# A graph network on one core: how four opening stages share their work among the engines

## The reference

```python
h = relu(layernorm(x))                                    # 625 x 512
# layer 0: mean of the neighbours, then one linear layer over [h, mean]
mean = segment_sum(h[src], dst, 625) / max(count, 1)
x = x + concat([h, mean]) @ W.T + b
# layer 1: two relational convolutions; layer 2: equivariant messages; layer 3: edge MLP with tail
# layer 1's weights of an edge: comp0[edge_type] * edge_weight and comp1[edge_type] * edge_weight
```

## Time and profile before

| | us |
|---|---|
| median of 3 runs | 2427.84 |
| lowest, highest | 2423.5, 2429.47 |
| the profiled execution | 2443.93 |
| its span in the trace | 2442.2 |
| PE busy / DVE / ACT / POOL | 2087.2 / 1827.6 / 1417.6 / 1259.0 |
| mean granted TensorE clock | 0.934 of 2.4 GHz |

### The profile page before, as it was taken

How to read it: one execution, slowest core, us unless ns; L and a number is a source line. 1 busy time by engine, 2 the same in 40 slices (tenths; PEclk the granted TensorE clock), 3 DMA queues, 4 the chain that set the end, 5 groups by cost and what they waited for, 6 DMA issues and landing times. The chain is left out here.

```text
span 2442.2 us, 38939 instructions
## 1 busy us (share of the span) xinstructions
PE 2087.2 (85%) x11291; PEld 1137.6 (47%) x11410; DVE 1827.6 (75%) x3717; ACT 1417.6 (58%) x2251; POOL 1259.0 (52%) x1060
## 2 busy tenths in 40 slices
PE   0567568888998886999999998799999999999965
PEld 0334257764665553444444445345555554555422
DVE  8658979965333344999999984699999999999723
ACT  2558667742112222444444442699999999999731
POOL 0572367741881004333333311588888888888530
PEclk9758889988999996999999999999999999999987
DMA  3310010010214324433333311332222222222000
GB/s 127 142 27 8 0 53 0 0 56 30 75 40 120 110 73 149 122 94 99 88 89 99 93 36 53 111 111 76 76 74 77 73 77 73 75 75 74 12 0 21
DMA packets 81554, 170.20 MB, mean 70 GB/s; under 512 B 17379, under 2 KB 43222, under 8 KB 80450
## 3 DMA queue, kind: packets, MB, share of 16 engines
q0 software_dynamic: 35840, 98.88, 14.9%
q1 hardware_dynamic: 45624, 70.25, 8.7%
HBM read 144.93 MB, written 23.98 MB: 69 GB/s over the span
## 5 line engine op out<-in xcount | busy, mean ns | idle before, releaser
L831 PE MATMUL e_two_ps<-w,e_first 128*128 128x512 bf16 x1342 | 407.8, 382 | 4.1 <-issue 0.2
L593 POOL DMA_INDIRECT sorted_records<-edge_record,slot_row x160 | 209.9, 1312 | 123.8 <-POOLq L731 60.2
L831 PE MATMUL e_two_ps<-w,e_first_low 128*128 128x512 bf16 x685 | 261.9, 382 | 0.6
L1678 POOL TENSOR_TENSOR e_first_low<-e_first 128x1024 bf16<-128x1024 f32 x88 | 250.3, 2844 | 21.8 <-DVE e_first L1869 21.8
L1683 POOL TENSOR_TENSOR e_msg_low<-e_act 128x1024 bf16<-128x1024 f32 x88 | 225.8, 2566 | 58.0 <-DVE e_act L1881 56.8
L1515 ACT ACTIVATE u_msg<-u_t,slot_record 128x128 f32<-128x128 f32 x528 | 172.9, 391 | 97.7 <-DVE u_t L1554 88.3
L2174 POOL DMA_INDIRECT e_got<-src_table,e_idx x176 | 186.7, 1061 | 70.4 <-POOL e_idx L2168 34.8
L1434 POOL DMA_INDIRECT u_got<-up_table,u_idx x176 | 168.9, 960 | 76.8 <-issue 42.9
L831 PEld LDWEIGHTS e_two_ps<-w,e_first 128*128 128x128 bf16 x1408 | 134.9, 98 | 150.2 <-issue 4.9
L1480 PE MATMUL u_sum_ps<-u_msg,u_hot 128*125 128x512 f32 x352 | 189.8, 621 | 15.4 <-DVE u_msg L1571 14.8
L635 PE MATMUL pairs_ps<-cell_high,src_hot 128*128 128x144 bf16 x1180 | 154.1, 228 | 43.7 <-POOL cell_rest L659 22.0
(11 more groups left out here) (349 smaller groups left out, 5275.3 us busy)
## 6 DMA issues: line engine op xcount, KB each, us to landing
conv_w<-in_L_gnn_basis_dram SPq DMA_DIRECT2D x8, 1024.0 KB
sorted_records<-pairs SPq DMA_DIRECT2D x5, 1408.0 KB, 10.9
edge_record<-in_edge_floats_dram SPq DMA_DIRECT2D x2, 3125.0 KB
later_w<-in_L_gnn_W_dram SPq DMA_DIRECT2D x6, 1024.0 KB
attr_parts<-h SPq DMA_DIRECT2D x22, 256.0 KB, 2.1
e_attrT<-attr_parts SPq DMA_DIRECT2D x44, 128.0 KB
e_dst_all<-dst_row SPq DMA_DIRECT2D x44, 125.0 KB
pairs<-in_edge_floats_dram SPq DMA_DIRECT2D x1, 3125.0 KB
```

The lines of the kernel that those rows point to most:

```text
L593: pg.nc.gpsimd.indirect_dma_start(out=pg.sorted, out_offset=bass.IndirectOffsetOnAxis(ap=pg.slot_row[:, j:j + 1], axis=0), in_=pg.edge_rec ...
L831: last = nc.tensor.matmul(out, lhsT, rhs, start=(n == 0), stop=(n == len(pairs) - 1))
L1678: nc.gpsimd.tensor_tensor(first_low[:, r % 2, 2 * u:2 * u + 2, :], full, upper(full), ALU.subtract).then_inc(low1, 1)
```

## The change

It has four parts. In place_edges the sum over buckets is done by 40 fused instructions and a tree of additions, two of its additions on POOL, ahead of POOL's work on the weights; the block tables move to POOL. In order_pairs the clearing of `pairs` is begun later and shared in other proportions, the coefficients' high parts are made on ACT, their rests on DVE, and the statistics of `x` are taken there. In build_pairs ACT makes `h`. In layer0 there is one block, and the counts, the means and the transposes of `h` work on bf16 halves.

```diff
@@ place_edges, POOL
+            pool.wait_ge(sem["group_compared"], 1)
+            nc.gpsimd.tensor_tensor(group_past[:, 0:2, :], group_past[:, 0:2, :], group_past[:, 2:4, :],
+                                    ALU.add).then_inc(sem["group_compared"], 1)
...
+            pool.wait_ge(sem["quarter_slots"], 2)
+            nc.gpsimd.tensor_tensor(pg.bucket_slot[:, 0:QUARTER, :], pg.bucket_slot[:, 0:QUARTER, :],
+                                    pg.bucket_slot[:, QUARTER:2 * QUARTER, :], ALU.add).then_inc(sem["slots_added"], 1)
+            pool.wait_ge(sem["slots_added"], 1)
+            pool.wait_ge(sem["quarter_slots"], 3)
+            nc.gpsimd.tensor_tensor(pg.bucket_slot[:, 0:QUARTER, :], pg.bucket_slot[:, 0:QUARTER, :],
+                                    pg.bucket_slot[:, 2 * QUARTER:3 * QUARTER, :], ALU.add)\
+                .then_inc(sem["slots_added"], 1)
@@ place_edges, ACT: the copies of the edge ends (late_ends) move behind the weights
@@ place_edges, DVE
-            link(nc.vector.tensor_tensor(rank[:, :, :], rank[:, :, :], over_j(shift[0:EP, :]), ALU.add))
-            link(nc.vector.tensor_tensor(pg.bucket_slot[:, :, :].rearrange("p j b -> p b j"), rank[:, :, :],
-                                         mine[:, :, :], ALU.mult))
-            link(nc.vector.tensor_reduce(slot[:, :], pg.bucket_slot[:, :, :], AX.X, ALU.add))
+            for b in range(BUCKETS):
+                last = nc.vector.scalar_tensor_tensor(out=pg.bucket_slot[:, b, :], in0=rank[:, b, :],
+                                                      scalar=shift[0:EP, b:b + 1], in1=mine[:, b, :],
+                                                      op0=ALU.add, op1=ALU.mult)
+                if b % QUARTER == QUARTER - 1:
+                    last.then_inc(sem["quarter_slots"], 1)
+            dve.wait_ge(sem["quarter_slots"], BUCKETS // QUARTER)
+            dve.wait_ge(sem["slots_added"], 2)
+            link(nc.vector.tensor_tensor(pg.bucket_slot[:, 0:QUARTER, :], pg.bucket_slot[:, 0:QUARTER, :],
+                                         pg.bucket_slot[:, 3 * QUARTER:4 * QUARTER, :], ALU.add))
+            left = QUARTER
+            while left > 2:
...
-            link(nc.vector.tensor_scalar(group_blk[:, :], group_no[:, :], last_group[:, 0:1], None, ALU.is_ge))
...
-            link(nc.vector.tensor_scalar(reached[:, :], item_last[:, :], pg.lane_no[:, 0:1], None, ALU.is_le))
-            nc.vector.tensor_reduce(bucket_of[:, :], reached[:, :], AX.X, ALU.add).then_inc(sem["tables_made"], 1)
@@ (these two now stand behind item_last, one compare for all blocks behind last_group)
@@ order_pairs, POOL
-            pool.wait_ge(placed, 1)
+            pool.wait_ge(decoded, 1)
...
-            for n in range(1, 4):
+            for n in range(1, 3):
                 nc.gpsimd.memset(pairs[:, n * size:(n + 1) * size], 0.0)
-            pool.wait_ge(high_early, 1)
-            nc.gpsimd.tensor_tensor(pg.pair_rest[:, :, 0:BASES].rearrange("p t n -> p n t"), coef[:, :, :],
-                                    pg.pair_high[:, :, 0:BASES].rearrange("p t n -> p n t"), ALU.subtract)
@@ order_pairs, ACT
+            act.wait_ge(x_var, 1)
+            nc.scalar.sqrt(x_sd[:, :], x_sd[:, :]).then_inc(x_root, 1)
             act.wait_ge(pg.emptied, 16 * 5)
...
+            nc.scalar.activation(pairs[:, 3 * size:], pg.ones[:, 0:1].broadcast_to([P, size]), ACT.Copy, scale=0.0)
             for m in range(2):
+                act.wait_ge(coefs_made, m + 1)
+                at = slice(2 * m, 2 * m + 2)
+                nc.scalar.copy(pg.pair_high[:, :, at].rearrange("p t n -> p n t"), coef[:, at, :]).then_inc(high_early, 1)
                 act.wait_ge(terms_read, 2 * (RELS - 1) + m + 1)
                 nc.scalar.copy(pg.pair_high[:, :, BASES + 2 * m:BASES + 2 * m + 2], later_coefs(m)).then_inc(high_late, 1)
@@ order_pairs, DVE
+            dve.wait_ge(pg.x_in, 16)
+            for b in range(NB):
+                last = nc.vector.bn_stats(out=pg.x_stats[:, b, :], in_=pg.x[:, b, :])
...
+            nc.vector.tensor_scalar(x_sd[:, :], x_mv[:, :, 1], EPS, None, ALU.add).then_inc(x_var, 1)
             dve.wait_ge(placed, 1)
...
+            for n in range(BASES):
+                last = nc.vector.tensor_scalar(coef[:, n, :], masks[:, first, :], ...)
+            link(last)
+            dve.sem_inc(decoded, 1)
             for r in RELS_IN_ORDER[2:]:
                 mask(r)
...
+            for m in range(2):
+                for k, r in enumerate(RELS_IN_ORDER[1:]):
+                    for n in range(2 * m, 2 * m + 2):
...                                         # scalar_tensor_tensor as before, linked after each pair
+            for m in range(2):
+                at = slice(2 * m, 2 * m + 2)
+                dve.wait_ge(high_early, m + 1)
+                nc.vector.tensor_tensor(pg.pair_rest[:, :, at].rearrange("p t n -> p n t"), coef[:, at, :],
+                                        pg.pair_high[:, :, at].rearrange("p t n -> p n t"), ALU.subtract)
@@ build_pairs, ACT, behind the last operand
+            for b in range(NB):
+                nc.scalar.activation(pg.h[:, b, :], pg.x[:, b, :], ACT.Relu, bias=pg.x_nmr[:, b:b + 1],
+                                     scale=pg.x_rs[:, b:b + 1])
@@ layer0
-        normalize(pg, "n0", sp_work=load, pe_work=counts, halves=True)
...
+                accumulate(nc, mean_ps[b % 2][:, :], [
+                    pair for sb in range(NB) for pair in three_products(
+                        linked_columns(0, sb, b), linked_columns(1, sb, b), h_parts[0][:, sb, :], h_parts[1][:, sb, :])])\
+                    .then_inc(made, 1)
+            def turn(b):
+                if b >= 2:
+                    pe.wait_ge(h_high, b - 1)
+                    pe.wait_ge(h_taken, b - 1)
+                for a in range(2):
+                    for f in range(4):
+                        last = nc.tensor.transpose(h_ps[b % 2][:, a, f, 0:BN], h_parts[a][:, b, f * P:(f + 1) * P],
+                                                   pg.ident16[0:BN, 0:BN])
+                last.then_inc(h_turned, 1)
...
+            pe.wait_ge(counts_early, 1)
+            pe.wait_ge(counts_late, 1)
+            for b in range(NB):
+                accumulate(nc, count_ps[:, b:b + 1], [(linked_columns(a, sb, b), pg.ones16[0:BN, :])
+                                                      for sb in range(NB) for a in range(2)]).then_inc(counted, 1)
+            pe.wait_ge(h_low, 1)
             mean(0)
+            for b in range(NB):
+                turn(b)
@@ layer0, ACT copies the high half of each turned block, DVE the low half (h_turned_low)
@@ layer0, POOL and DVE: the low half of the count matrix, 2 and 3 of its 5 sets; DVE: the low half of h
+            nc.gpsimd.tensor_tensor(linked[1][:, at, :], pg.pairs[0:BN, at, COEFS, :], linked[0][:, at, :],
+                                    ALU.subtract).then_inc(counts_late, 1)
...
+            nc.vector.tensor_tensor(linked[1][:, at, :], pg.pairs[0:BN, at, COEFS, :], linked[0][:, at, :],
+                                    ALU.subtract).then_inc(counts_early, 1)
+            nc.vector.tensor_tensor(h_parts[1][:, :, :], pg.h[:, :, :], h_parts[0][:, :, :], ALU.subtract).then_inc(h_low, 1)
```

More of the change, by code:

```diff
@@ L78, in constants @@
     pg.before = pg.sb("before", [P, P])
+    pg.ones16 = pg.sb("ones16", [P, 1], BF16)
     pg.ln2 = pg.sb("ln2", [P, 1])
@@ L251, in _ @@
                 nc.scalar.copy(pg.weight_part[:, n, :], weight_16[:, n, :]).then_inc(sem["weight_part"], 1)
+            for n, at in ((0, slice(0, EARLY)), (1, slice(EARLY, EC))):
+                ends = pg.late_ends if n else pg.edge_record[0:EP, 0:EARLY, SRC:SRC + 2]
+                nc.scalar.copy(ends[:, :, 0], ints[:, 0, at])
+                nc.scalar.activation(ends[:, :, 1], ints[:, 1, at], ACT.Identity, bias=pg.ones[0:EP, 0:1])
         @block.tensor
@@ L564, in _ @@
             link(nc.vector.tensor_copy(pg.pair_high[:, :, COEFS], filled[:, :]))
+            first = RELS_IN_ORDER[0]
+            dve.wait_ge(x_root, 1)
+            nc.vector.reciprocal(pg.x_rs[:, :], x_sd[:, :]).then_inc(x_chain, 1)
+            dve.wait_ge(x_chain, 3)
+            nc.vector.scalar_tensor_tensor(out=pg.x_nmr[:, :], in0=x_mv[:, :, 0], scalar=-1.0, in1=pg.x_rs[:, :],
+                                           op0=ALU.mult, op1=ALU.mult)
+            dve.wait_ge(comp_in, 32)
+            for n in range(BASES):
+                last = nc.vector.tensor_scalar(coef[:, n, :], masks[:, first, :],
+                                               comp[:, 0, first * BASES + n:first * BASES + n + 1], None, ALU.mult)
+            link(last)
+            dve.sem_inc(decoded, 1)
             for r in RELS_IN_ORDER[2:]:
@@ L993, in _ @@
             for b in range(NB):
+                act.wait_ge(h_turned, b + 1)
+                nc.scalar.copy(hT[:, 0, :, nodes_of(b)], h_ps[b % 2][:, 0, :, 0:BN]).then_inc(h_high, 1)
+            for b in range(NB):
```

(2 more changed lines are left out.)

124 lines of the change are left out of this document (76 added, 48 removed).

## The result

| | before | changed |
|---|---|---|
| median, us (4 runs each) | 2426.38 | 2406.47 |
| lowest, highest | 2423.5, 2429.47 | 2405.49, 2410.63 |
| ratio, with 95% interval | | 0.9921 [0.9903, 0.9939] |
| span of the profiled execution | 2442.2 | 2404.3 |
| mean granted clock in it | 0.934 | 0.947 |

A forecast was written before the change was run, and what follows sets the result against it. Each block was taken to cost what its last engine needs: DVE in place_edges, ACT behind the loop, PE in the first layer. 4.9 + 8.7 - 0.95 + 4.4 = 17.0 us off 2427.84 gave 2410.8, range 2400 to 2420.

The forecast's parts named there:

- place_edges: Sum over buckets: DVE stays the bound, POOL's additions add to its time, DVE ends at 65.05, 4.9 us saved.
- The carry through the loop: order_pairs' loop: begun earlier, it ends earlier by as much, so place_edges' 4.9 us carry through.
- Behind the loop: End of order_pairs: ACT is late, its second clearing on the path; block ends at 309.2, 8.7 us saved.
- build_pairs: ACT's five added relus end 0.95 us behind DVE; cost 0.95 us, 1.7 at most.
- layer0: First layer, timed from its start T: product(0) ends at T + 33.2, later means shorter; 4.4 us saved.
- The rule on transposes: First layer: transposes don't count as busy for the clock gate, so the clock falls and mean(1) costs 6.0 us.
- The first: Rival, first layer: clock stays up through counts, mean and transposes, saving 11.3 us; 2403.9 us, chance 0.15.
- The second: Rival, order_pairs: POOL's memsets hold back DVE's masks, pair_cell and coefficients; 2415.7 us, chance 0.16.
- The third: Rival, place_edges: POOL's additions cost L442's price, block ends 2.2 us later than before; 2417.9 us, chance 0.08.
- The fourth: Rival, first layer: the one block doesn't shorten it; 2415.2 us, chance 0.11.
- the slower one: Rival, first layer: PE stays at the low clock, 7.4 us more a block, 2452 us with all five; chance 0.03.
- my own mark: First layer: the prediction called itself wrong if product(0) ended before T + 30, T being the layer's start.

The follow-up runs named there:

- e5: The changed kernel with POOL's two additions of slots (1600 elements each) done by DVE instead; 2406.92 us, ratio to before 0.9926.
- e1: The kernel before, unchanged, profiled a second time, on another chip; 2382.67 us (1 run).
- e2: The kernel before with the changed place_edges alone; 2380.27 us, ratio to before 0.9996.
- e3: The changed kernel with the clearing of before: three memsets on POOL once the slots are placed, one clearing on ACT; 2365.18 us, ratio to before 0.9941.
- e4: The changed kernel with the old first layer and norm, without statistics of x in order_pairs or relu in build_pairs; 2366.37 us, ratio to before 0.9941.
- e0: The changed kernel again, no edit, on a later chip; 2407.26 us, ratio to before 0.9929.
- e8: The changed kernel with early high copies and rests of the coefficients walked in the outputs' memory order; 2403.04 us, ratio to before 0.9915.
- e11: The changed kernel with the first layer's 50 bf16 count products issued six times over; 2411.74 us (1 run).
- e7: The changed kernel with each block of h transposed three times over, 24 bf16 transposes instead of 8; 2407.20 us (1 run).
- e6: The changed kernel with the last quarter of the clearing moved from ACT to POOL, three memsets there; 2398.29 us, ratio to before 0.9891.

## Why the prediction was right, and where it wasn't

The time and its range held (2406.5 in 2400 to 2420, forecast 2410.8), and the direction. Step by step:

- **place_edges.** Right, to 0.45 us. The terms came out (12.0 and 11.92; two additions on POOL, 7.8 forecast, 3.4 and 3.56 once they ran; 65.05 and 65.48 at the end), because the two engines' times were added and not overlapped. e5 shows what that means: the shared work is worse than DVE alone, by 2.05 us.
- **The carry through the loop.** Against e1 the loop ends 4.7 us earlier in e2, 4.1 in e3 and 3.8 in e4, where it began 4.6, 4.35 and 4.3 earlier. On the other kind of chip the loop's length differs by 5 us from one execution of the changed kernel to the next, and only one profile of the kernel before is there; whether all 4.45 us arrive there is open. The stretches without the loop give 4.45 + 5.8 - 0.8 + 12.15 = 21.6 us; the medians 19.9 and 17.5 (e0). The 2 to 4 us between are unsettled.
- **Behind the loop.** The path was right (through ACT, second clearing on it, copies begin at 285.96, 32.5 us after the slots as forecast). The size of the term "four copies at 0.95 us, two rests at 0.86" was wrong: 6.06 us and, for the rests behind the last copy, 2.46 us. I had taken rows whose outputs I hadn't looked at for their order. In e8, with the outputs in the order of memory, the stretch is 4.1 us shorter. So 5.8 instead of 8.7 us.
- **build_pairs.** +0.8, forecast +0.95.
- **layer0.** The step that failed: 12.15 us instead of 4.4. Its terms: the counts (T + 11.0 forecast for their end, T + 6.0 found; they and DVE's halves together are 3.3 us, since the counts are hidden behind L1147 and cost 0.030 us each and not the 0.108 of an fp32 pass); mean(0) 0.8 shorter, as the clock rose within it (its 5.8 us has no working in the prediction, 15 x 0.427 is 6.4; in e11, at the low clock nearly throughout, it took 5.72); the turns 0.4; mean(1) with product(0) behind it 2.6 shorter, as the clock did not fall again; the three later means 0.6. That is 7.7 of 7.75. Up to 1.4 us of the 12.15 may not be the change's: the old layer itself took 72.2 to 73.6 us.
- **The rule on transposes** that I weighed with mean(1) decided wrongly: where it made the fall "sure", the granted clock stayed 1.00 through the turns, and in e7 through 6.87 us of 120 transposes. The Trainium skill, "TensorE: Matmul & The Clock Gate", Part 4, says that full speed doesn't engage for transposes; no run here shows a fall behind one, and whether transposes can raise the clock was not tested.
- **Rivals.** The first (the clock stays up) came true in its second half: low in counts and mean(0), full from there on; its 2403.9 is 2.6 us off, nearer than the forecast's 2410.8 (4.3). The second, POOL's memsets holding two-input steps, is refuted by e6 and the 4.08 and 12.08 us rows. The third, slow additions on POOL: the record of 9.24 us looks like it but is waiting. The fourth and the slower one did not occur. By my own mark, product(0) before T + 30, I was wrong on layer0, and two errors of opposite sign (2.9 us too much behind the loop, 7.75 too little in layer0) let the sum look better than its parts. That the time fell where it did is in part luck.

## What to carry to other kernels

Before an elementwise step is shared between DVE and POOL, look which kind it is beside what runs on the other engine: where DVE's step has two inputs in SBUF and POOL's reads SBUF, their times add, and POOL's rate makes the help a loss (2 us here), while POOL's memsets can be laid beside DVE's two-input steps for nothing (e6, 7 us), but not beside its TENSOR_SCALARs from SBUF (e3, 5.1 us lost net). Take the price of a copy from a row with the same order of elements in the output, not only the same count. A piece that is moved to another block is paid there: charge it (4.3 + 0.8 us of the norm) before counting the gain of the block it left.

## What the runs showed of the hardware

- A stream of back-to-back DVE steps with two SBUF inputs kept POOL's read-type addition out for its whole length, not for one step: POOL asked at 45.78 and got through only after the last of the forty, 5.8 us later, though DVE had some twenty instructions' ends in between.
- The same program's loop under POOL's indirect DMAs took 142.3 us on one chip and 196.7 on another, with short "issue" stops of PE and a granted clock of 0.58 instead of 1.00 on the second. The changed kernel's loops on the second kind of chip (183.4 to 188.3 us) lie 41 to 46 us above the loops on the first, and the kernel before differs by 43 us in its medians: nearly all of the difference between the chips is this loop. What causes it is open.
- 300 one-column bf16 products at the low clock cost 0.028 us each, and after 181 of them PE stood 3.38 us on "issue". Why wasn't tested.
